# Macaron block on one core: X1 statistics one iteration earlier, keys before queries, normalised X2 rows after the exponentials

## The reference

```python
x = x + 0.5 * ffn(layernorm(x))
x = x + attention(layernorm(x))
x = x + 0.5 * ffn(layernorm(x))

def attention(x):            # 16 heads of 32
    q, k, v = split_heads(x @ Wq.T + bq), split_heads(x @ Wk.T + bk), split_heads(x @ Wv.T + bv)
    q, k = jnp.exp(q), jnp.exp(k)
    kv = jnp.cumsum(k[:, :, :, None] * v[:, :, None, :], axis=1)
    k1 = jnp.cumsum(k, axis=1)
    out = jnp.einsum('zsD,zsDd->zsd', q, kv) / jnp.sum(q * k1, axis=-1, keepdims=True)
    return merge_heads(out) @ Wo.T + bo

def ffn(x):                  # 32 experts, each picks 8 tokens of a sequence
    probs = softmax(x @ gate_w.T + gate_b, over experts)
    vals, idx = top_k(probs over tokens, 8)
    merged = sum over the 8 tokens of vals * x[idx]
    o = gelu(merged @ w1[:-1] + w1[-1]) @ w2[:-1] + w2[-1]
    return zeros.at[idx].add(vals * o)
```

## Time and profile before

| | us |
|---|---|
| median of three runs | 2307.36 (2302.71 to 2310.95) |
| the profiled execution's own time | 2305.76 |
| its span | 2304.0 |
| attention: first to last KT copy | 961.6 to 1648.7 |
| TensorE busy over the span | 1952.8 (85%) |
| ScalarE, VectorE, GpSimd busy | 814.9, 731.5, 607.2 |

### The profile page before, as it was taken

How to read it: one execution, slowest core, us unless ns; L and a number is a source line. 1 busy time by engine, 2 the same in 40 slices (tenths; PEclk the granted TensorE clock), 3 DMA queues, 4 the chain that set the end, 5 groups by cost and what they waited for, 6 DMA issues and landing times.

```text
span 2304.0 us, 43710 instructions
## 1 busy us (share of the span) xinstructions
PE 1952.8 (85%) x18472; PEld 1159.4 (50%) x18472; DVE 731.5 (32%) x1206; ACT 814.9 (35%) x1525; POOL 607.2 (26%) x744
## 2 busy tenths in 40 slices
PE   5789999999999999998999999999876556656576
PEld 4546666666666666666676676676621111111111
DVE  6631111111111111477767667666411000000011
ACT  6831111121121122476777777777610000000000
POOL 7610000000000000265676676676402000000002
PEclk9989999999999999999999999999997878787877
DMA  9999999999999999684766665666499999999997
GB/s 364 352 378 403 419 399 429 428 425 421 428 419 426 419 422 395 165 276 165 264 230 205 234 225 200 201 238 211 156 412 424 428 401 427 428 428 428 428 427 334
DMA packets 130626, 798.53 MB, mean 347 GB/s; under 512 B 30072, under 2 KB 30200, under 8 KB 89728
## 3 DMA queue, kind: packets, MB, share of 16 engines
q1 hardware_dynamic: 114880, 711.59, 77.9%
q10 hardware_dynamic: 9216, 50.34, 5.3%
q0 software_dynamic: 6336, 33.81, 3.8%
HBM read 674.02 MB, written 132.59 MB: 350 GB/s over the span
## 4 chain that ended last, share of the span: by engine, by line
PE 49%; DMA 24%; POOL 12%; ACT 6%; issue 5%; DVE 2%; SPq 2%; POOLq 0%; ACTq 0%; DVEq 0%
PE ps L345 46%; DMA big<-in_L_ffn_w 22%; POOL big L1569 2%; POOL s L1554 2%; POOL s L1572 2%; POOL big L1543 2%; SPq L18 2%; PE ps L349 2%; ACT big L1381 1%; DMA last_scratch<-idx 1%; ACT big L631 1%; POOL big L1566 1%; ACT big L616 1%; PE ps L820 1%; POOL big L1548 1%
## 5 line engine op out<-in xcount | busy, mean ns | idle before, releaser
L345 PE MATMUL ps<-big 128*32 128x512 f32 (+4 forms) x13600 | 950.1, 412 | 234.1 <-DMA big<-in_L_ffn_w 188.2
L345 PEld LDWEIGHTS ps<-big 128*32 128x32 f32 (+2 forms) x13600 | 376.4, 126 | 730.9 <-issue 379.1
L353 DVE TENSOR_TENSOR big<-ps,big 128x2048 f32<-128x2048 f32 (+4 forms) x291 | 277.8, 960 | 712.7 <-PE ps L820 510.9
L345 PE MATMUL ps<-wth,xth 128*128 128x512 f32 x768 | 311.8, 406 | 1.5 <-DVE xtl L353 1.5
L345 PE MATMUL ps<-wtl,xth 128*128 128x512 f32 x768 | 299.6, 390 | 0.0
L345 PE MATMUL ps<-wth,xtl 128*128 128x512 f32 x768 | 299.3, 390 | 0.0
L868 ACT COPY big<-ps 128x512 f32<-128x512 f32 x64 | 37.5, 586 | 648.3 <-PE ps L345 648.3
L1561 POOL TENSOR_SCALAR big<-big 128x1 f32<-128x1 f32 x64 | 17.3, 270 | 843.4 <-ACT ps L1359 830.7
L1011 ACT ACTIVATE big<-ps,big 128x512 f32<-128x512 f32 x128 | 88.2, 689 | 371.8 <-PE ps L345 359.3
L1020 DVE TENSOR_SCALAR big<-ps,big 128x512 f32<-128x512 f32 x64 | 48.1, 751 | 533.7 <-PE ps L345 533.7
L345 PE MATMUL ps<-wo,s 128*128 128x512 f32 x768 | 210.0, 408 | 2.6 <-ACT s L1426 1.4
(11 more groups left out here) (139 smaller groups left out, 1766.6 us busy)
## 6 DMA issues: line engine op xcount, KB each, us to landing
big<-in_L_ffn_w SPq DMA_DIRECT2D x254, 2048.0 KB, 18.7
p_weight_x_scratch<-big ACTq DMA_DIRECT2D x64, 768.0 KB, 11.0
big<-p_weight_x_scratch SPq DMA_DIRECT2D x64, 768.0 KB, 6.3
xt_scratch<-big SPq DMA_DIRECT2D x16, 1024.0 KB, 8.5
big<-xt_scratch SPq DMA_DIRECT2D x16, 1024.0 KB, 15.6
x_weight_scratch<-big SPq DMA_DIRECT2D x64, 256.0 KB, 3.3
out_x<-big SPq DMA_DIRECT2D x64, 256.0 KB, 4.5
big<-in_L_attn_x SPq DMA_DIRECT2D x15, 1024.0 KB, 10.9
```

The lines of the kernel that those rows point to most:

```text
L345: return nc.tensor.matmul(o, l, r, start=start, stop=stop, skip_group_check=True)
L353: return nc.vector.tensor_tensor(o, p, q, op)
```

## The change

- The square of X1 and its sum for tiles 16 to 63 are made one iteration earlier: ScalarE after the values of n+1, VectorE after X1 + bo, GpSimd at the end of the arithmetic of the iteration, ahead of its gathers and scatters. Tiles 0 to 15 keep their places on VectorE and ScalarE.
- ScalarE makes the exponential of the keys, then KH, then the exponential of the queries. GpSimd makes KL and then the factor on the queries. This holds for all tiles.
- The normalised rows XN3 of n-2 stand behind the exponentials and KH of n+1, no longer ahead.
- Since the squares' junk output now goes to the buffer OS[1] for all tiles from 16, TensorE's wait for them ends at tile 16, and the load of the weight chunk 4E+3, whose place covers OS[1], moves from iteration 52 to 62 of SyncE's stream.

```diff
--- before.py
+++ after.py
@@ -1127,9 +1127,9 @@
                 if n == 16:
                     sp.wait_ge(s_c, 8 * TILED)
                     load_chunk(sp, 4 * E + 4)
-                if n == 52:
+                if n == NT - 2:
                     sp.wait_ge(s_gc, GC0 + NGR)
-                    sp.wait_ge(s_x1sq, NT - 12)
+                    sp.wait_ge(s_x1sq, NT)
                     load_chunk(sp, 4 * E + 3)
                 if n in (54, 58):
                     sp.wait_ge(d_s, 16 * NGR)
...
@@ -1336,6 +1336,12 @@
                         mm(ps[:, 0, :], h4(ATH)[:, g, :], WOL[:, g, :], False, False)
 
         def attention_act(act):
+            def square_act(t, junk):
+                act.wait_ge(s_x1, t + 1)
+                act.wait_ge(s_x1ve, t - 1)
+                nc.scalar.activation(junk, X1[t % 4], ACT.Square, bias=SX1[t % 2], scale=-float(D),
+                                     accum_out=SQ1[t % 2]).then_inc(s_x1sq, 1)
...
@@ -1351,13 +1357,8 @@
                 live = 0 <= n < NT
                 nxt = 0 <= n + 1 < NT
                 m, c = n + 1, n % 8
-                if nxt:
-                    act.wait_ge(s_x1, m + 1)
-                    act.wait_ge(s_x1ve, m - 1)
-                    if m == 8 * TILED:
-                        act.wait_ge(s_c, 8 * TILED)
-                    nc.scalar.activation(OS[1] if 8 * TILED <= m < NT - 12 else ps[:, 7, :], X1[m % 4], ACT.Square,
-                                         bias=SX1[m % 2], scale=-float(D), accum_out=SQ1[m % 2]).then_inc(s_x1sq, 1)
+                if nxt and m < 8 * TILED:
+                    square_act(m, ps[:, 7, :])
...
@@ -1366,6 +1367,20 @@
                     act.wait_ge(s_qtT, n + 1)
                     act.wait_ge(s_av, n)
                     nc.scalar.copy(QT, ps[:, 1, :]).then_inc(s_qt, 1)
+                if nxt:
+                    act.wait_ge(*((s_tqv, m + 1) if m < 8 * TILED else (d_pb[m % 4], 16 * (m // 4 + 1))))
+                    act.wait_ge(s_x1rs, m + 1)
+                    if m < 8 * TILED:
+                        act.wait_ge(s_tk, m + 1)
+                    nc.scalar.activation(PB[m % 4][:, 1, :], PB[m % 4][:, 1, :], ACT.Exp,
+                                         scale=RS[m % 2]).then_inc(s_ke, 1)
+                    act.wait_ge(s_ke, m + 1)
+                    act.wait_ge(s_wol, 1)
+                    act.wait_ge(s_upto, m)
+                    act.wait_ge(s_after, kvs(m))
+                    nc.scalar.copy(KH, PB[m % 4][:, 1, :]).then_inc(s_kh, 1)
+                    nc.scalar.activation(PB[m % 4][:, 0, :], PB[m % 4][:, 0, :], ACT.Exp,
+                                         scale=RS[m % 2]).then_inc(s_qe, 1)
                 if 0 <= n - 2 < NT:
                     t = n - 2
                     act.wait_ge(s_nm, t + 1)
@@ -1375,20 +1390,6 @@
                         act.wait_ge(s_mtok, 8 + (t - NX) // 8 + 1)
                     nc.scalar.activation(XN3[t % NX], X2, ACT.Identity, bias=NM[t % 2],
                                          scale=RS[2 + t % 2]).then_inc(s_x2n, 1)
...
-                if nxt:
-                    act.wait_ge(*((s_tqv, m + 1) if m < 8 * TILED else (d_pb[m % 4], 16 * (m // 4 + 1))))
-                    act.wait_ge(s_x1rs, m + 1)
-                    nc.scalar.activation(PB[m % 4][:, 0, :], PB[m % 4][:, 0, :], ACT.Exp,
-                                         scale=RS[m % 2]).then_inc(s_qe, 1)
-                    if m < 8 * TILED:
-                        act.wait_ge(s_tk, m + 1)
...
-                    nc.scalar.copy(KH, PB[m % 4][:, 1, :]).then_inc(s_kh, 1)
                 if n >= 11 and c == 3:
                     topk_exp(act, 8 + (n - 11) // 8)
                 if 0 <= n - 2 < NT:
@@ -1398,6 +1399,9 @@
                 if nxt:
                     nc.scalar.activation(PB[m % 4][:, 2, :], PB[m % 4][:, 2, :], ACT.Identity,
                                          scale=RS[m % 2]).then_inc(s_v, 1)
+                if 8 * TILED <= n + 2 < NT:
+                    act.wait_ge(s_c, 8 * TILED)
+                    square_act(n + 2, OS[1])
                 if n >= 12 and c == 4:
                     merge_transpose_act(act, 8 + (n - 12) // 8, 1)
                 if 0 <= n - 1 < NT:
@@ -1491,10 +1495,9 @@
                 if live and n + 1 < NT:
                     state_dve(n + 1)
                 m = n + 2
-                if m < NT:
+                if m < 8 * TILED:
                     dve.wait_ge(d_x1[m % 4], 16 * (m // 4 + 1))
                     dve.wait_ge(s_x1sq, m - 1)
-                if m < 8 * TILED:
...
-                elif m < NT:
-                    nc.vector.tensor_reduce(SX1[m % 2], X1[m % 4], AX.X, ALU.add).then_inc(s_x1, 1)
...
@@ -1516,19 +1517,33 @@
                     dve.wait_ge(s_bo2, 1)
                     dve.wait_ge(s_x1sq, m + 1)
                     tt(X1[m % 4], X1[m % 4], BO, ALU.add).then_inc(s_x1b, 1)
+                m = n + 3
+                if 8 * TILED <= m < NT:
+                    dve.wait_ge(d_x1[m % 4], 16 * (m // 4 + 1))
+                    dve.wait_ge(s_x1sq, m - 1)
+                    nc.vector.tensor_reduce(SX1[m % 2], X1[m % 4], AX.X, ALU.add).then_inc(s_x1, 1)
         def attention_pool(pool):
+            def scale_pool(t):
+                pool.wait_ge(s_x1sq, t + 1)
+                nc.gpsimd.tensor_scalar(VE[t % 2], SQ1[t % 2], 1.0 / D ** 3, EPS, ALU.mult,
+                                        ALU.add).then_inc(s_x1ve, 1)
+                pool.wait_ge(s_x1ve, t + 1)
+                for s_ in (s_ke, s_qe, s_v):
+                    pool.wait_ge(s_, t - 1)
+                nc.gpsimd.tensor_tensor(RS[t % 2], VE[t % 2], NHALF, ALU.pow).then_inc(s_x1rs, 1)
+
             pool.wait_ge(s_bo2, 1)
             pool.wait_ge(s_eb, 1)
             for n in range(-2, NT + 1):
                 m = n - 1
                 if 0 <= m < NT:
                     pool.wait_ge(s_x2sq, m + 1)
-                    pool.wait_ge(s_kl, min(n + 2, NT))
+                    pool.wait_ge(s_qb, min(n + 2, NT))
...
@@ -1555,21 +1570,19 @@
                 m = n + 2
                 if m < NT:
                     j = m % 4
-                    pool.wait_ge(s_x1sq, m + 1)
                     pool.wait_ge(s_atl, n + 1)
                     pool.wait_ge(s_qn, n + 2)
-                    nc.gpsimd.tensor_scalar(VE[m % 2], SQ1[m % 2], 1.0 / D ** 3, EPS, ALU.mult,
-                                            ALU.add).then_inc(s_x1ve, 1)
-                    pool.wait_ge(s_x1ve, m + 1)
-                    for s_ in (s_ke, s_qe, s_v):
-                        pool.wait_ge(s_, m - 1)
-                    nc.gpsimd.tensor_tensor(RS[m % 2], VE[m % 2], NHALF, ALU.pow).then_inc(s_x1rs, 1)
+                    if m < 8 * TILED:
+                        scale_pool(m)
+                    pool.wait_ge(s_kh, m + 1)
+                    pool.wait_ge(s_x1rs, m + 1)
+                    nc.gpsimd.tensor_tensor(KL, PB[j][:, 1, :], KH.bitcast(F), ALU.subtract).then_inc(s_kl, 1)
                     pool.wait_ge(s_qe, m + 1)
-                    pool.wait_ge(s_x1rs, m + 1)
+                    pool.wait_ge(s_kl, m + 1)
                     nc.gpsimd.tensor_tensor(PB[j][:, 0, :], PB[j][:, 0, :], BK, ALU.mult).then_inc(s_qb, 1)
-                    pool.wait_ge(s_kh, m + 1)
-                    pool.wait_ge(s_qb, m + 1)
-                    nc.gpsimd.tensor_tensor(KL, PB[j][:, 1, :], KH.bitcast(F), ALU.subtract).then_inc(s_kl, 1)
+                if 8 * TILED <= n + 3 < NT:
+                    pool.wait_ge(s_qb, n + 3)
+                    scale_pool(n + 3)
                 if turn(n, 0):
                     rows_gather_pool(pool, turn(n, 0))
                 for i in range(2):
```

10 lines of the change are left out of this document (2 added, 8 removed).

## The result

The changed kernel takes 2330.48 us (median of four runs, 2324.58 to 2334.25) against 2305.59 us (2302.71 to 2310.95) of the kernel before on the same chip: a ratio of 1.0098, 95% interval 1.0079 to 1.0118. It is slower, by 22.6 us if the ratio is taken (the medians differ by 24.9). The forecast was 2325.

A forecast was written before the change was run, and what follows sets the result against it. No attention engine is full; waits set the step of about 10.9 us, and its loss passes to the end. Terms -2.5 + 7.2 + 2.8 + 10 = +17.5 us on 2307.4 gave 2325 us; 8-in-10 range 2295 to 2340.

The forecast's parts named there:

- late steps without DMAs: Attention from tile 16: KL waits go but XN3 comes later; 0.2 us gained per step with n%8 = 4, 6: -2.5 us.
- behind the late gathers: Four steps after late gathers: GpSimd's DMAs wait behind the scale, delaying the queries' division; 1.7 to 1.9 each, +7.2 us.
- scatters: Late steps with a scatter behind GpSimd's scale: n%8 = 2 fits in, n%8 = 3 loses 0.7 in each of four: +2.8 us.
- early tiles: Tiles 0 to 15: XN3 behind the exponentials leaves TensorE idle 1.3 us before its transposes; +10 us, bounds 0 and 20.
- port, moved load: VectorE and GpSimd meeting at the memory port, and the 2 MB weight chunk loaded at about 1640 us: both 0.
- granted clock: TensorE's clock level in the attention: the forecast had no term for it.
- the plain ones: Early steps 1 to 4 and 10, where the attention was to come 0.95 us later in each: 4.8 us.
- The lower bound of this term: Late steps' best case: all of TensorE's KL waits go and nothing follows, -20.5 us.
- Rival 1: Late steps: KL really came last, so its waits go and steps shrink to 10.0 us; 2290 us, chance 0.22.
- Rival 2: ScalarE's queue in late steps: the square delays X2 statistics and division by 0.4 each; 2340 us, chance 0.15.
- Rival 3: Nothing on the path: VectorE's work covers the early loss, slack the gathers; within 0.3%, 2307 us, chance 0.13.
- The expert stage: Second expert stage, starting when the attention ends: forecast to take 641 us as before.

The follow-up runs named there:

- fill: Changed kernel plus constant-tile transposes on TensorE in iterations 0 to 14 and late iterations n%8 = 2 and 3: 2329.73 us, ratio 1.0117 to the kernel before.
- dma_first: Changed kernel with GpSimd's gathers and scatters put back ahead of the X1 scale: 2320.49 us, ratio 1.0057 to the kernel before.
- early_behind: Kernel before with XN3 moved behind KH in iterations 0 to 14 only: 2320.53 us, ratio 1.0055.
- xn3_first: Changed kernel with ScalarE's XN3 put back ahead of the exponentials in all iterations: 2316.02 us, ratio 1.0043 to the kernel before.
- S: Part of the change: X1 statistics one iteration ahead; alone on the kernel before, ratio 0.9981.
- K: Part of the change: keys ahead of queries on ScalarE and GpSimd; alone on the kernel before, ratio 1.0045.
- both: Changed kernel with XN3 back ahead of the exponentials and gathers and scatters back ahead of the scale: 2309.60 us, ratio 1.0005 to the kernel before.
- stats_only: Kernel before with X1 statistics one iteration ahead and late gathers and scatters behind the scale: 2308.33 us, ratio 1.0017.
- keys_only: Kernel before with only keys put ahead of queries on ScalarE and GpSimd: 2314.09 us, ratio 1.0045.
- stats_dma: Kernel before with only the X1 statistics one iteration ahead, gathers and scatters staying ahead of the scale: 2298.23 us, ratio 0.9981.
- after_again: Changed kernel, unchanged, profiled once more: attention 713.4 us, against 713.0 in its first profile.
- before_again: Kernel before, unchanged, profiled once more: attention 686.8 us, against 687.1 in its first profile.
- stats_fill: Kernel before with X1 statistics one iteration ahead, plus constant-tile transposes ahead of the state-update wait in late iterations n%8 = 2 and 3: 2295.47 us, ratio 0.9955.
- X: Part of the change: XN3 behind the exponentials; by the ratios it costs 0.0052 (12.0 us) from the kernel with XN3 and DMAs moved back.
- D: Part of the change: GpSimd's gathers and scatters behind the scale; added to the statistics one iteration ahead, it costs 0.0036 (8.3 us).

## Why the prediction was right

The forecast was right in sign and 5 us short of the measured median. In the terms of its sum, with what the first profile has for each:

```
                                   forecast   measured
late steps without DMAs              - 2.5      - 2.3   (n%8 = 7: -4.8; 1: +1.0; 53, 54, 61, 62: +1.4)
behind the late gathers              + 7.2      + 7.0   (step and the one behind it, four times)
scatters                             + 2.8      + 2.3   (in n%8 = 3 and mostly 4)
early tiles                          +10        +10.3   (as in fill and dma_first, without low clock)
port, moved load                       0          0     (divisions 69.9 us in all, before 73.4; from the last KT copy to the end 655.1, before 655.2)
granted clock                        none       + 8.6   (4.8 early, 3.8 late: an upper bound)
sum                                  +17.5      +25.9
```

*Early tiles.* The mechanism is shown: early_behind makes 7.7 us of the loss with XN3's place alone, and xn3_first takes nearly all of it away. With S and K there, XN3's place is worth 9.0 (dma_first against the kernel both, neither with a low clock in these steps), and the 1.4 that are left come without it. The single steps were not right. I had 0.95 for each of the plain ones and measured 0.5 to 0.7 in steps 3, 4 and 10 and -0.3 in step 1; 5, 13 and 14 and, unforeseen, 12 with 1.4 had more. The sum came out by errors that cancel.

*Late gathers.* The division started 11.5 behind the KT copy where I had 11.3, and the size is right. But that it is all the DMAs' place is not. That place is worth 0.9 to 1.3 us per gather (dma_first, stats_only); the kernels keys_only and both have 0.9 to 1.0 of their own in the same steps without it. In keys_only, with the queries' product behind KL, the gather starts 7.4 to 7.6 behind the KT copy, where it was 6.4 before, and the division at 10.9 to 11.1. In the kernel called both the gather starts at 6.5, but the scale stands behind it, and the division starts at 10.9 as well. I had counted one cause for what two make. How the stall of the weight loads, which the kernel both has and keys_only has not, shares in this is open.

*Scatters.* The 0.7 each is what stats_only shows (0.65 to 0.7), one step later than I had it. Against before it half hides, since S alone makes steps 20 and 28 0.55 us shorter. In the changed kernel it is not as clear: with the DMAs back ahead of the scale (dma_first) step 36 is 0.65 shorter, while step 20 is the same.

*Late steps.* The sum is near, the place again not. I gave the gain to steps with n%8 = 4 and 6. It lies in n%8 = 7, mostly 0.75 us each. stats_dma has the same without K, and keys_only has 0.56 to 1.27 in four of these six steps (23, 31, 39, 47) without S; in the two others only S has it. So either edit gives most of it, and the two do not add up. The lower bound of this term took all 20.5 us of waits for KL as late ones; 5.7 of them lie in the early steps.

*The clock.* This is the step that is missing. I worked out how much longer TensorE would wait and not what the length of one wait does to it. Both profiles of the changed kernel have the lower level for 20 us and more of the attention. What it costs is known early: steps 0 and 2 take 4.6 us less where no stretch is in them (dma_first, fill). The late 3.8 are too many: step 43 is 0.8 over before in after_again without a stretch, and that leaves about 3.0.

Why it falls is in part argued. What the profiles show of the late steps is this. In the four without an idle piece of TensorE of 1.4 us or more (before, before_again, early_behind, stats_fill, none over 1.32) no stretch lies there; in the ten others, with 7 to 16 such pieces each, there are 1 to 7. stats_fill takes the pieces away and the stretches go. But a long piece isn't enough: fill's late part has sixteen of 1.45 to 1.8 us and a single stretch, dma_first has the changed kernel's piece of 1.9 us in step 2 and no fall, and early_behind has one of 2.1. Nor is it always needed: the stretch at 1452.47 comes behind waits of 0.5 us and less. What else decides stays open.

*Rivals.* Rival 1 (faster, KL came last) is refuted by keys_only, where most of the wait goes and the time grows. There was something to gain in S: 4 us by the ratio, 6 in the profile, without K, X and D. Rival 2 (the square of X1 delays that of X2) isn't seen: in stats_fill, with the square in that very place, step 27 alone of the late steps is longer than before, and it holds a wait of 2.8 us for the load of X1. Rival 3 is out by the interval. The expert stage and the moved load were as forecast.
